# Attention in sixteen groups of four heads by 256 queries, with the weighted sums of two key tiles at the end of a step

## What is computed

```python
def _L0_attn_ref(x, Wqk_w, Wqk_b, Wv_w, Wv_b, Wo_w, Wo_b):
    qk = (x @ Wqk_w.T + Wqk_b).reshape(b, n, H, E, 2)
    q = jnp.transpose(qk[..., 0], (0, 2, 1, 3))
    k = jnp.transpose(qk[..., 1], (0, 2, 1, 3))
    v = (x @ Wv_w.T + Wv_b).reshape(b, n, H, E)
    v = jnp.transpose(v, (0, 2, 1, 3))
    scores = jnp.einsum('bhqd,bhkd->bhqk', q, k)
    attn = jax.nn.softmax(scores, axis=-1) / jnp.asarray(HEAD_DIM ** 0.5, x.dtype)
    out = jnp.einsum('bhsl,bhlv->bhsv', attn, v)
    out = jnp.transpose(out, (0, 2, 1, 3)).reshape(b, n, H * E)
    return out @ Wo_w.T + Wo_b

def _L0_ffn_ref(x, gate_q, gate_s, up_q, up_s, down_q, down_s):
    Wg = dequant(gate_q, gate_s)
    Wu = dequant(up_q, up_s)
    Wd = dequant(down_q, down_s)
    gate_score = jax.nn.silu(jnp.einsum('bsh,ih->bsi', x, Wg))
    intermediate = gate_score * jnp.einsum('bsh,ih->bsi', x, Wu)
    return jnp.einsum('bsi,hi->bsh', intermediate, Wd)

x = _layernorm(x + _L0_attn_ref(x, ...), axis=-1)
x = _layernorm(x + _L0_ffn_ref(x, ...), axis=-1)
```

## Time and profile before

| | |
|---|---|
| median of 3 runs | 528.93 us (528.42 to 530.14) |
| the profiled execution | 530.17 us, span 528.2 us |
| TensorE busy | 505.1 us (96%), granted clock 0.991 of full |
| DVE busy | 414.5 us (78%) |
| ACT busy | 408.6 us (77%) |
| POOL busy | 246.9 us (47%) |
| first scores of the second pass | 51.60 us |
| first gate matmul | 220.53 us |

### The profile page before, as it was taken

One profiled execution on the slowest core, in us unless ns is written; L12 is line 12 of the kernel. 1 busy time (PEld: TensorE's weight loads), 2 busy tenths in 40 slices (PEclk: granted clock), 3 DMA queues, 4 the chain that ended last, 5 costly groups with the idle time before them and its releaser, 6 DMA issues.

```text
span 528.2 us, 8092 instructions
## 1 busy us (share of the span) xinstructions
PE 505.1 (96%) x2984; PEld 194.3 (37%) x2984; DVE 414.5 (78%) x706; ACT 408.6 (77%) x562; POOL 246.9 (47%) x287
## 2 busy tenths in 40 slices
PE   9899899999999999999999999999999999999991
PEld 3222223323323222334444444444444444444440
DVE  3698999989999996378787877876666866668777
ACT  1542688999899989866888888888888888888860
POOL 9000073824100715065656569385463583642864
PEclk9999899999999999999999999999999999999997
DMA  6400007576540006310312202102000002000022
GB/s 189 163 18 7 20 21 201 186 142 136 78 70 2 2 5 159 150 50 1 60 22 40 41 1 51 30 2 80 1 0 1 0 2 79 2 1 1 0 81 79
DMA packets 29687, 28.69 MB, mean 54 GB/s; under 512 B 19408, under 2 KB 21584, under 8 KB 29392
## 3 DMA queue, kind: packets, MB, share of 16 engines
q1 hardware_dynamic: 26224, 22.14, 14.5%
q0 software_dynamic: 3424, 6.03, 6.2%
HBM read 24.10 MB, written 4.22 MB: 54 GB/s over the span
## 4 chain that ended last, share of the span: by engine, by line
PE 86%; DVE 8%; ACT 4%; issue 1%; POOLq 0%; DVEq 0%; POOL 0%; ACTq 0%
PE ps L1076 18%; PE ps L1064 18%; PE ps L1091 17%; PE ps L1008 9%; PE ps L979 6%; PE ps L900 6%; DVE mxh L1181 3%; PE ps L831 3%; ACT pbuf L700 2%; PE ps L991 2%; PE ps L956 2%; PE ps L885 1%; PE ps L841 1%; PE ps L1018 1%; DVE st L1211 1%
## 5 line engine op out<-in xcount | busy, mean ns | idle before, releaser
L1181 DVE TENSOR_REDUCE mxh<-ps 128x1 f32<-128x512 f32 x256 | 157.4, 682 | 9.3 <-PE ps L900 8.2
L700 ACT ACTIVATE pbuf<-ps,gamma 128x1024 f32<-128x1024 f32 x128 | 141.6, 1113 | 19.7 <-PE ps L979 14.8
L780 ACT ACTIVATE ps<-ps,ratio 128x512 f32<-128x512 f32 x168 | 106.5, 659 | 41.0 <-PE ps L1064 37.9
L1091 PE MATMUL ps<-wd,stack 128*128 128x512 f16 x448 | 131.6, 379 | 0.7 <-POOL stack L622 0.7
L1076 PE MATMUL ps<-arena,wu 128*128 128x512 f16 x448 | 115.3, 379 | 1.0 <-DVE pbuf L1325 1.0
L1341 DVE TENSOR_TENSOR ps<-ps,stack 128x512 f32<-128x512 f32 x128 | 88.1, 695 | 35.1 <-PE ps L1091 33.8
L1064 PE MATMUL ps<-arena,wg 128*128 128x512 f16 x448 | 115.5, 379 | 0.1
L786 ACT ACTIVATE ps<-ps,ratio 128x512 f32<-128x512 f32 x156 | 98.9, 659 | 6.1 <-PE ps L1076 1.6
L620 POOL CAST stack<-pbuf 128x512 f16<-128x512 f32 x56 | 34.1, 609 | 94.2 <-DVE pbuf L1325 94.2
L1341 DVE TENSOR_TENSOR ps<-ps,pbuf 128x512 f32<-128x512 f32 x80 | 55.3, 697 | 26.0 <-PE ps L1091 25.6
L1008 PE MATMUL ps<-pbuf,arena 128*32 128x256 f32 x832 | 67.3, 395 | 1.7 <-ACT avt L707 1.7
(11 more groups left out here) (111 smaller groups left out, 380.3 us busy)
## 6 DMA issues: line engine op xcount, KB each, us to landing
arena<-xT SPq DMA_DIRECT2D x16, 256.0 KB, 5.8
x<-x SPq DMA_DIRECT2D x2, 2048.0 KB, 9.7
out<-x SPq DMA_DIRECT2D x3, 1024.0 KB, 4.2
stack<-down_ratios SPq DMA_DIRECT2D x1, 2048.0 KB, 7.4
wg<-gq POOLq DMA_DIRECT2D x4, 448.0 KB, 7.3
wu<-uq POOLq DMA_DIRECT2D x4, 448.0 KB, 7.3
wd<-dq POOLq DMA_DIRECT2D x2, 896.0 KB, 11.1
pbuf<-down_ratios SPq DMA_DIRECT2D x1, 1536.0 KB, 6.4
```

What stands on the lines that cost most here:

```text
L700: nc.scalar.activation(pbuf[:, pi % 4, :].rearrange("p (a n) -> p a n", a=2), ps[:, at:at + 2, :], ACT.Exp, scale=gamma[:, n // (ALL // B) ...
L780: nc.scalar.activation(gbank[t % 2], gbank[t % 2], ACT.Copy, scale=gr[:, t % G, c:c + 1])\
L1091: mm = nc.tensor.matmul(bank[k], mparts[:, a, t % NM, k * P:(k + 1) * P], wd[:, i, :], start=(i == 0 and a == 0), stop=(a == 1), skip_grou ...
L1181: nc.vector.tensor_reduce(mxh[:, f % 2, qh, half:half + 1], ring_bank("first", n), AX.X, ALU.max)\
```

## The change

A group becomes four heads by 256 queries, sixteen groups (`NF`), and a step two key tiles of such a group (`KS` = 4 steps a group, again 64 steps). A pair's scores are four matmuls of 256 columns. The weighted sums of both key tiles of step n - 1 are issued together behind everything else of step n, sixteen instructions. `AHEAD` is 30 units, so that the first pass ends in step 56. The turns of maxima are 16 (step 4f - 3), each with four DMAs of a head's part; the turns of the sums have two transposes instead of four. The q rows of the second half of batch 0 are no longer placed by TensorE and kept by ACT but by eight DMAs of SP, with one memset on POOL. The tail has seven uses of the ring's banks in place of eleven (output projections in pairs), and other orders on DVE, POOL and SP follow from that; the weights and the bias come in smaller parts. `STATS_AT` and `RESULT_AT` move.

```diff
-NG = H // HG
-STEPS = NG * KT
+QB = 2
+QT = BT // QB
+QN = TB // QB
+GROUPS = H // HG * QB
+NF = NB * GROUPS
+KS = KT // 2
+STEPS = GROUPS * KS
 ALL = NB * STEPS
-FG = HG * BT * 2
-FIRST = NB * NG * FG
+MQ = HG * QT
+FG = 2 * MQ
+FIRST = NF * FG
 AHEAD = FG + 14
...
-        DRAIN = ALL - 11
-        aside = [("attT", 1, 0), ("wo", 1, 0), ("wo", 1, 1), ("wo", 1, 2), ("avT", LASTF, 0), ("wo", 1, 3),
-                 ("attT", 2, 0), ("wo", 2, 0), ("wo", 2, 1), ("wo", 2, 2), ("wo", 2, 3)]
+        DRAIN = ALL - 7
+        ASIDE = {DRAIN: ("attT", 1, 0), DRAIN + 1: ("wo", 1, 0), DRAIN + 2: ("wo", 1, 1), DRAIN + 3: ("attT", 2, 0),
+                 DRAIN + 4: ("wo", 2, 0), DRAIN + 5: ("avT", LASTF, 0), DRAIN + 6: ("wo", 2, 1)}
...
-        placed = [use for t in range(TH) for use in ((1, 0, t), (0, 0, t), (1, 1, t))] + [(0, 1, t) for t in range(TH)]
+        placed = [use for t in range(TH) for use in ((1, 0, t), (0, 0, t), (1, 1, t))]
...
-        STATS_AT = {1: 2, 2: 8, 3: 15}
-        RESULT_AT = [p + 6 for p in ended.values()]
+        STATS_AT = {1: 5, 2: 12, 3: 19}
+        RESULT_AT = (26, 34, 48)
...
+            def place_second_half():
+                for jj in range(2):
+                    for part in range(2):
+                        for slot in range(4)[half_slots(0, part)]:
+                            r = ROWS * jj + E * slot
+                            src = (high, low)[part][jj * HD // 2:(jj + 1) * HD // 2, TB:2 * TB]
+                            sp.dma_start(qs[0][r:r + E, 1, :, :], src).then_inc(s_half, 16)
...
-                for jj in range(2):
-                    r = ROWS * jj + MROW
-                    sp.dma_start(qs[b][r:r + 3, k, 2 * g:2 * g + 2, :],
-                                 mrows[6 * BT * jj:6 * BT * (jj + 1), f % 2, :]).then_inc(s_mld[g], 16)
+                for c in range(HG):
+                    r, t = ROWS * (c // 2) + MROW, 2 * g + c % 2
+                    sp.dma_start(qs[b][r:r + 3, k, t, h * QN:(h + 1) * QN],
+                                 mrows[3 * QT * c:3 * QT * (c + 1), f % 2, :]).then_inc(s_mld[q4], 16)
...
             max_rows(1)
+            max_rows(2)
...
             place_rows(sp, 1)
             sp.dma_start(x1[:, 0:8, :], x[0:8].rearrange("t p n -> p t n")).then_inc(s_x[0], 16)
-            max_rows(2)
+            max_rows(3)
+            max_rows(4)
...
-                for j in range(2):
-                    rows, t = slice(ROWS * j, ROWS * (j + 1)), 2 * g + pair
-                    mm = nc.tensor.matmul(bank[at + j], ks[b][rows, t, kt * P:(kt + 1) * P],
-                                          qs[b][rows, k, t, :], start=True, stop=True)
+                for kk in range(2):
+                    kt = 2 * kp + kk
+                    for j in range(2):
+                        rows, t = slice(ROWS * j, ROWS * (j + 1)), 2 * g + pair
+                        mm = nc.tensor.matmul(bank[at + j][:, kk * QN:(kk + 1) * QN], ks[b][rows, t, kt * P:(kt + 1) * P],
+                                              qs[b][rows, k, t, h * QN:(h + 1) * QN], start=True, stop=True)
...
-                lo, hi = half * TB // 2, (half + 1) * TB // 2
                 for j in range(HG):
-                    mm = nc.tensor.matmul(bank[AVB][j * VC:(j + 1) * VC, lo:hi], vst[b][:, kt, g * HG + j, :],
-                                          pbuf[:, (2 * n + j // 2) % 4, (j % 2) * TB + lo:(j % 2) * TB + hi],
-                                          start=(kt == 0 and half == 0), stop=(kt == KT - 1), skip_group_check=True)
+                    lo = (j % 2) * TB + kk * QN
+                    mm = nc.tensor.matmul(bank[AVB][j * VC:(j + 1) * VC, h * QN:(h + 1) * QN], vst[b][:, kt, g * HG + j, :],
+                                          pbuf[:, (2 * n + j // 2) % 4, lo:lo + QN],
+                                          start=(kt == 0), stop=(kt == KT - 1), skip_group_check=True)
...
                     for use in turns_at(n, pair):
                         turn(*use)
+                for kk in range(2):
                     if n:
-                        av(n - 1, pair)
+                        av(n - 1, kk)
...
+            for k in range(2):
+                row_maxima(0, k)
+            combine_tops(0)
...
+                if n == 24:
+                    row_maxima(1, 0)
...
             mean_variance(0)
             att_out(1)
+            normalise(LASTF - 1)
+            for t in range(2):
+                add_output(1, t)
+            apply(0)
+            for t in range(2, BT):
+                add_output(1, t)
             down_ratios()
-            add_output(1, 0)
-            apply(0)
-            add_output(1, 1)
-            add_output(1, 2)
```

More of the change, by code:

```diff
@@ L193, in build @@
         s_mrow = sem("max_parts_ready")
-        s_mld = [sem(f"max_rows_in_stack{g}") for g in range(NG)]
+        s_mld = [sem(f"max_rows_in_stack{g}") for g in range(GROUPS)]
         s_scf = sem("scores_full")
@@ L448, in turn_x1 @@
                         .then_inc(s_x1t[u], 16)
-            for f in range(4, NB * NG):
+            for f in range(5, NF):
                 max_rows(f)
-                if f == 5:
+                if f == 10:
                     sp.wait_ge(s_scf, 2 * ALL // B)
@@ L542, in load_weights @@
             def load_weights(f):
[L544 to L554, removed]
+                pool.wait_ge(s_mld[f % GROUPS], 16 * HG * (f // GROUPS + 1))
+                half, kind = (f - 4) % 2, (f - 4) // 2
+                if kind < 2:
+                    for c in range(2 * half, 2 * half + 2):
+                        pool.dma_start((wg, wu)[kind][:, c, :], (gq, uq)[kind][c]).then_inc(s_gu, 16)
+                else:
+                    own = slice(half * G // 2, (half + 1) * G // 2)
+                    pool.dma_start(wd[:, own, :], dq[own].rearrange("g p n -> p g n")).then_inc(s_dq, 16)
             split_max(0)
             split_max(1)
+            split_max(2)
             second_batch_parts()
+            split_max(3)
             pool.wait_ge(s_low, 3)
@@ L754, in _ @@
             place_v(0)
-            for n in range(4, 11):
+            for n in range(4, 7):
                 keep(n)
             project_qk(1, 0)
-            for n in range(11, 16):
-                keep(n)
+            keep(7)
+            keep(8)
             project_v(1)
             first_max_out()
+            keep(9)
+            keep(10)
             place_v(1)
+            keep(11)
             project_qk(1, 1)
@@ L766, in _ @@
                     exps(n, pair)
-                    if pair and n and n % KT == 0:
-                        av_out(n // KT - 1)
+                    if pair and n and n % KS == 0:
+                        av_out(n // KS - 1)
                     for use in turns_at(n, pair):
@@ L924, in turn @@
                 if (kind, u, k) in aside:
-                    i = aside.index((kind, u, k))
-                    if i >= 3:
-                        wait_aside_read(pe, aside[i - 3])
-                    else:
-                        wait_ring_read(pe, "first", FIRST - 1)
+                    wait_ring_read(pe, "first", FIRST - 1)
+                    for other in before_in_bank(kind, u, k):
+                        wait_aside_read(pe, other)
                     at = aside_bank(kind, u, k)
@@ L952, in turn @@
                         wait_attT(pe, u)
-                    single = (kind, u, k) in aside
-                    for j in (k % 2,) if single else range(2):
-                        rows, pick_k = slice(j * HD, (j + 1) * HD), k // 2 if single else k
-                        mm = nc.tensor.matmul(bank[at if single else at + j], attT[rows, pick_k * P:(pick_k + 1) * P],
-                                              wo_s[rows, :], start=True, stop=True)
+                    for j in range(2):
+                        rows = slice(j * HD, (j + 1) * HD)
+                        mm = nc.tensor.matmul(bank[at + j], attT[rows, k * P:(k + 1) * P], wo_s[rows, :],
+                                              start=True, stop=True)
                 mm.then_inc(s_of, 1)
@@ L1054, in _ @@
                     turn(*use)
-                av_whole(n - 1)
-            av_whole(ALL - 1)
+                for kk in range(2):
+                    av(n - 1, kk)
+            for kk in range(2):
+                av(ALL - 1, kk)
             def gate(t, c):
```

198 lines of the change are left out of this document (101 added, 97 removed).

## The result

The changed kernel takes 559.34 us (median of 6 runs, 558.2 to 562.83), the kernel before in the same runs 529.43 us (528.42 to 530.14): a ratio of 1.0576, 95% interval 1.0545 to 1.0607. It is slower by 30 us. The forecast was 547.1 us and its range, 532 to 568, holds the time. The side and the mechanism of the step were right; the loss was 18 us in the forecast and is 30.

What follows compares the result with a forecast made beforehand. DVE's row-maxima reductions were taken to set the attention's pace, with the merged burst making the bank loop longer. -4.7 + 31.1 - 6.9 - 1.3 = +18.2 us on 528.93 gave 547.1; own range 538 to 556, with rivals 532 to 568.

Steps and rivals of the forecast that it cites:

- the stretch: First scores to last reduction: 171.6 us, +31.1, from 56.5 steps of 2.73 us plus transposes, output projection, early steps and stall.
- the tail: Last reduction to first gate matmul: 21.6 us, -6.9, set by the transposes of x1 rather than the steps' 19.6.
- the head: Start to first scores: -4.7 us, bounds -2 and -5.5, from fewer first-pass matmuls and placements; first scores at 46.9.
- the feed-forward part: From the first gate matmul on: -1.3 us, as the statistics of block 1 leave period 3.
- The loop: Attention, reuse of three PSUM banks: 1.16 + 0.32 + 1.00 + 0.25 = 2.73 us a step against DVE's 2.40; bounds 2.68 and 3.10.
- B: Rival: TensorE's short pauses halve its clock in a quarter of the attention steps, +21 us, 568 us; chance 0.12.
- E: Rival: in each attention step four short score matmuls cost two pairs, +0.2 us x 56, 558 us; chance 0.07.
- A: Rival: DVE is not starved in the attention, so faster or the same, 525 to 528 us; chance 0.13.
- stall at group 3: Attention near 82 us: group 3's maxima wait behind SP's 2 MB load of x; 6.5 us, bounds 0 and 8.
- D: Rival: four DMA issues of maxima take longer than 0.74 us each, maxima 0.4 us late in 15 groups, 553; chance 0.08.
- C: Rival: the load of x doesn't hold the maxima up in the attention, 541 us; chance 0.20.
- The early steps: First steps of the attention after the first scores: 2.4 us beyond the normal step time.

Runs made afterwards that it cites:

- e4: The kernel before, with both halves of a step's weighted sums put at the step's end and nothing else changed: 544.5 us, ratio 1.0273.
- e8: The changed kernel with the second key tile's weighted sums issued twice, 24 matmuls in a burst (result not the block's): 581.9 us.
- e9: The changed kernel with the second key tile's weighted sums left out for all four heads, 8 matmuls in a burst (result not the block's): 547.1 us.
- e5: The changed kernel with burst split, x of batch 0 loaded early, group 3's maxima ahead of SP's placements, ratios behind the copy of block 1: 533.4 us, ratio 1.0084.
- e1: The changed kernel with the eight weighted sums of a key tile back behind their own pair, so the burst is cut in two: 551.2 us, ratio 1.0401.
- e2: The changed kernel with x of batch 0 loaded before the maxima of group 0: 552.32 us, ratio 1.0417.
- e3: The changed kernel with DVE's down ratios made right behind the statistics of block 0: 555.59 us, ratio 1.0485.

## Why the prediction was right or wrong

Against the profiled execution the forecast was 12.1 us too small: 5.9 in the stretch, 4.6 in the tail, 1.5 in the head and 0.1 in the feed-forward part.

*The loop: right.* 2.73 us a step forecast, 2.71 measured; burst 1.00 against 1.01, scores 0.25 against 0.22, DVE idle 0.3 against 0.23 once a step. e4 shows the cause by itself, e8 and e9 its slope and its lower end.

*The range: in part luck.* The forecast's own range was 538 to 556 us, and 559.34 lies outside it. The range of 532 to 568 holds it only by the room that it leaves for B and E. Neither happened; what filled that room were a stall and a tail that I had priced too low.

*Rivals.* A is out by e4, but its price for the stretch was fair. It gave a stretch of 152.5 us for groups of this kind at DVE's pace. e5 is such a kernel, and its stretch is 155.9 us with 1.8 us of stall in it; its tail is 20.2 us, where I had 19.6 from the steps alone. A gave 528 because it left out every stall at group 3. The same omission misled me in e1: I expected 539, without seeing that a group at this pace takes 10.88 us and that its maxima are due earlier. B, the clock by short pauses, did not happen: TensorE pauses 0.3 us in each step, and the clock is 1.00 in the window 160 to 170. What the prediction cites for it from the Trainium skill finds no support here. D and E did not happen (5.2 us for the maxima, 0.22 for the scores), nor did C.

*The step that failed first: the stall at group 3.* I took 6.5 us of 0 to 8. It is 10.05 (the scores were due at 85.56 and came at 95.61) and 1.7 for the half clock behind it (steps of 4.22 and 2.94 us in place of 2.71): 11.8, outside my bounds, and 5.3 of the 5.9 us by which the stretch was missed. I had priced only x's load, at 5.5 us, by a transfer of 0.5 KB behind 1 MB. Here the load ahead was 2 MB and landed 13.8 us after its issue (13.7 in the row is the median of both loads of x), and four transfers wait where it was one. The placements ahead on SP, which were in my text as the reason for x's time, I left out of this wait; by e2 and e5 at least 3 us of it are theirs, and 4 us are not the load's.

*The early steps.* Five steps take 17.4 us (48.39 to 65.81), where 5 x 2.71 + 2.4 is 16.0. The clock was 0.66 between 50 and 60 us in this execution and 1.00 in those of e1, e2 and e3. So this part is not fixed, and why it fell there was not tested. The turns came at 5.3 us in place of 6.2 (14 groups at 0.38). About 1 us of the stretch stays unassigned.

*The step that failed second: what is late next in the tail.* I named the transposes of x1, which gave 21.6 us. They took 24.2 (225.9 to 250.1) and were still in time, for the gate came after 26.2. Their term was too small mainly because the first of them began 16.9 us behind the last reduction, where my sum has 14.7: they wait for the ratios, which took 4.3 us and not 1.6 as in e3. The rest is a misreading of the earlier trace rows: four issues that cover 6.92 us start 1.9 us apart and not 1.23; after the change they start 1.4 apart. Late was TensorE's wait of 4.06 us for DVE's copy of turned attention, behind the ratios, with a granted clock of 0.66 in the window 240 to 250. I had counted the ratios as "two more additions ahead of the ratios that SP waits for", that is for SP alone, and not asked who else waits behind them on DVE. Nor had I seen that they would now run beside GpSimd's splitting. e3 took 3.1 us out of the tail.

*The head.* -4.7 forecast, -3.2 measured. I took eight pairs away at 0.32 each. The number of places for units among the other matmuls stayed at 23. Sixteen of them now hold one unit in place of two, and one alone costs as much as the pair in my sum: 27.24 to 27.56, 0.32 us.

*The feed-forward part.* -1.3 forecast, -1.2 measured.

## What to carry to other kernels

Where results go through a few banks to the engine that sets the pace, add up the path from one use to its reuse, with everything that stands in the producer's queue between them. Two bursts merged into one cost nothing in work and yet lengthen this path; here each us of burst was a us of step beyond 0.69. Before a group is halved, list what comes once per group on every queue, and for each small transfer what SP has in front of it. When a stall is moved, list everything that waits behind the moved instruction on its own engine, not only the one consumer that you have in mind.

## What the runs showed of the hardware

*DVE beside GpSimd.* The operation on the scales behind these, of the same 128 x 112 fp32 form and with both operands in SBUF, took 0.28 us in the kernel after, where GpSimd did nothing (241.99), and 1.26 us in e3, where GpSimd's tensor operation of 1.16 us had begun 0.03 us before it (239.04 and 239.07); it ended 0.13 us after that one. In the fence on the tail 238.13 and 238.16 show the same pair. The reciprocal of 128 x 56, with one operand, took 0.50 us beside GpSimd's work (after, 239.45) and 0.51 in e3. The Trainium skill has this in "SBUF — State Buffer", section "SBUF: two separate sides": the port pair that the two share is a lock held for the whole instruction, and a DVE operation with two SBUF inputs contends for it. These rows agree. Worked from rows, the five instructions of the ratios lost 2.7 us of DVE time in the tail, 2.45 of it in the three with two SBUF inputs (0.73, 1.26 and 1.20 us for 0.24, 0.28 and 0.22). One pair does not fit: in e3, at 227.33, the DVE operation took its 0.28 us although GpSimd's operation of 128 x 4 had begun at 227.28 and its record is 1.04 us long. Records of GpSimd are rough, and why this one held nothing up stays open.

*Matmuls in column tiles.* Twelve in 0.99 us, sixteen in 1.01, eight in 0.57, twenty-four in 1.44. The first eight cost 0.57 and each further eight 0.43 to 0.44; so some 0.14 us of a burst are its own, and merging two saves about that much.

*The clock.* After 10 us of waiting it was at the lower of its two levels (0.50 in the window 90 to 100, 1.2 GHz), and after 4 us in the tail too (four output projections in 2.08 us; those at 229.35 took 1.13). In e3 it was at that level after a wait of 1.55 us, with TensorE busy 1.35 of the 2.9 us before 228.9, that wait included. In the middle of the attention, where TensorE pauses 0.3 us in each step, it was 1.00.
